# A recommendation tower on one core: a third table split into halves, the first dense part and one batch of transposes moved, the gather indices loaded on another queue

## The chip, the cores and the metric

One core of one Trainium2 chip runs the kernel. The metric is the device time of one execution in microseconds (us).

## The reference

512 samples each take one row of 128 floats from each of 26 tables, and have one dense vector of 128 features. The 27 vectors of a sample are multiplied with each other pairwise (351 dots), and dense vector and dots go through three layers.

```python
e = jnp.stack([tbl_0[ids[:, 0]], ..., tbl_25[ids[:, 25]]], axis=1)
ss = jnp.einsum('bfd,bgd->bfg', e, e); sd = jnp.einsum('bfd,bd->bf', e, dense)
z = concatenate([dense, sd, ss[:, iu, ju]], axis=1)           # iu, ju: pairs above the diagonal
h = concatenate([z, dense], axis=1)                            # 607 columns
h = maximum(h @ W_top1 + b_top1, 0)                            # 512
h = maximum(h @ W_top2 + b_top2, 0)                            # 256
y = h @ W_top3                                                 # 1
```

## The kernel before

The kernel holds the looked-up vectors transposed, as embT: 128 dimensions on the partitions, then sample, then slot (27 slots, padded to 32).

Twelve of the tables (1000 or 1250 rows) are looked up by a product with a one-hot matrix. Each of them is loaded whole over SP's DMA queue (load_table), ACT rounds it to fp32r (the high part, split_high, L324), DVE takes the remainder (the low part, split_low, L386) and compares the indices with each of 8 (once 10) chunk numbers (onehot, L378), and TensorE adds up 16 (once 20) products of a chunk's high and low part with the one-hot columns (L472). Buffers for table, high, low, onehot and the PSUM result exist three times (STAGES). ACT then copies the result into its slot of embT (L335). The step of a table is called T0 to T11; the semaphore table_selected counts finished products, table_placed the copies into embT.

The other 14 tables are gathered by GpSimd with an indirect DMA each, for each of 4 tiles of 128 samples: 56 gathers, numbered k = 14 t + n, into rows (two buffers, for even and odd tiles). k up to 42 are also paced by table_selected, and gathers named in HELD_BY_DOTS wait until the dots of an earlier tile are done. What is gathered is transposed by TensorE four tables at a time (the batches B t.b, L507; the last batch of a tile has two tables), and ACT or DVE copies a batch from PSUM into embT (L308, L371).

Then, for each tile t: TensorE makes the dots (D t, L527, 128 products); ACT and DVE copy them from PSUM into pairs, 22 copies each, in two parts of 11 (C t.0 and C t.1, L308 and L371); the first layer is the dense part (P t, 8 products, L543) and the pairs part (L t.0, L t.1, L552, 32 products); ACT applies the relu (R t, L349); the second layer (M t, L569), its relu (H t, on ACT and DVE), the third (Y t, L576) and the copy of the result (V t) follow. D t waits for all copies of C t-1, since the dots of all tiles share four PSUM banks, and for the batches of its tile in embT.

Every engine walks the same written list (STEPS) and does its part of each step, in order; between engines there are semaphores alone. A table with an entry in `late` is split: its first 256 samples are selected in step T t.0 ahead of D0, the other 256 in steps T t.1 to T t.4 (L485, 16 products) behind D0, into a PSUM region of their own, and ACT copies that half into embT in step A t (L338). Before, this holds for the last two tables (10 and 11). Table 10's late half goes to last_layers, table 11's to half of hidden[1].

Before the tables, TensorE runs some warming products, and spread_ids copies the indices of a table to all partitions with a product (L445).

Of the kernel before, what the change touches and what calls it, by code (L numbers as in the profile page):

```python
# [31 lines left out]
N_ONEHOT = len(ONEHOT_TABLES)  # L32
# [17 lines left out]
def dlrm_tower(nc, gather_ids, onehot_ids, spread, tables, dense_t, w_pairs, w_dense, small, w2, identity,  # L50
# [9 lines left out]
    GATHERS_AHEAD, GATHERS_PER_TABLE = 4, 3  # L60

    LATER_GATHERS = GATHERS_AHEAD + GATHERS_PER_TABLE * (N_ONEHOT + 1)
    HELD_BY_DOTS = {39: 1, 46: 2, 51: 3}
    WARMING = 29
    WARMING_BETWEEN = 6
    CHUNKS1 = HIDDEN1 // 128
# [3 lines left out]
    with ctx:  # L70
        def sb(name, shape, dt=F32):
            return ctx.enter_context(nc.sbuf_tensor(name, shape, dt))

        def pb(name, shape):
            return ctx.enter_context(nc.psum_tensor(name, shape, F32))

        def sem(name):
            return ctx.enter_context(nc.semaphore(name))

        gather_idx = sb("gather_idx", [128, TILES, N_GATHERED], I32)  # L80
# [26 lines left out]
        hidden = [pb(f"hidden{i}", [128, CHUNKS1, TILE]) for i in range(2)]  # L107
        last_layers = pb("last_layers", [128, 512])
        HALF_BATCH = BATCH // 2
# [2 lines left out]
        relative = banks[2:4]  # L112
        selected = [banks[0], banks[1], hidden[0].rearrange("p a b -> p (a b)")]

        late = {N_ONEHOT - 2: last_layers[:, 0:HALF_BATCH],
                N_ONEHOT - 1: hidden[1][:, 0:2, :].rearrange("p a b -> p (a b)")}

# [5 lines left out]
        gather_ids_loaded = sem("gather_ids_loaded")  # L124
# [19 lines left out]
        table_placed = sem("table_placed")  # L144
# [30 lines left out]
        def lows_to(i, chunk):  # L175

            return 2 * i + 1 + chunk // half(i)

        def loads_of(i):
# [3 lines left out]
        NAMES = {"T": "table", "D": "dots", "C": "copies", "B": "batch", "P": "dense", "L": "layer1", "R": "relu1",  # L183
                 "M": "layer2", "H": "relu2", "Y": "layer3", "V": "result", "A": "late half"}
        STEPS = [(NAMES[w[0]], *map(int, w[1:].split("."))) for w in """
            T0 T1 B0.0 T2 B0.1 T3 T4 B0.2 T5 B0.3 T6 B1.0 T7 B1.1 T8 B1.2 T9 B1.3 T10.0 T11.0 B2.0
            D0 C0.0 T10.1 T10.2 T10.3 T10.4 A10 T11.1 T11.2 T11.3 T11.4 C0.1 P0 B2.1 B2.2 A11
            D1 C1.0 B2.3 L0.0 L0.1 R0 C1.1 P1 B3.0 M0 H0
            D2 Y0 C2.0 V0 B3.1 L1.0 L1.1 R1 C2.1 P2 B3.2 M1 H1 B3.3
            D3 Y1 C3.0 V1 L2.0 L2.1 R2 C3.1 P3 M2 H2  # L190
            L3.0 Y2 V2 L3.1 R3 M3 H3 Y3 V3""".split()]
# [12 lines left out]
        def batch_placer(n):  # L204
            return PLACERS[n]
# [10 lines left out]
        @block.sync  # L216
        def _(sp):
            def load_rows(i, first, last, done):
                rows_of_part = tables[ONEHOT_TABLES[i]][:, :].rearrange("(p c) d -> p c d", c=CHUNKS[i])
                for a, b in ROW_PIECES:  # L220
                    sp.dma_start(table[i % TABLE_BUFFERS][a:b, first:last, :], rows_of_part[a:b, first:last, :]
                                 ).then_inc(done, 16)

            def load_table(i):
                if i >= TABLE_BUFFERS:
                    sp.wait_ge(low_ready, lows_to(i - TABLE_BUFFERS, CHUNKS[i - TABLE_BUFFERS] - 1))
                load_rows(i, 0, CHUNKS[i], table_loaded[i % TABLE_BUFFERS])

            def load_weights(n):
                dst, src = MLP_LOADS[n]  # L230
                sp.dma_start(dst, src).then_inc(mlp_loaded, 16)

            sp.dma_start(spread_f[0:ID_ROWS, :], spread).then_inc(spread_loaded, 16)
            for n, (first, last) in enumerate(parts(0)):
                load_rows(0, first, last, first_loaded[n])
            load_table(1)
            load_table(2)
            sp.dma_start(ident[:, :], identity).then_inc(ident_loaded, 16)
            load_table(3)
            load_table(4)  # L240
            sp.dma_start(denseT[:, :], dense_t).then_inc(dense_loaded, 16)
            load_table(5)
            for i in range(6, N_ONEHOT):
                load_table(i)
                if i - 6 < len(MLP_LOADS):
                    load_weights(i - 6)
            sp.wait_ge(y_ready, TILES)
            sp.dma_start(out, y).then_inc(stored, 16)
            sp.wait_ge(stored, 16)

        @block.gpsimd
        def _(pool):
# [4 lines left out]
            for t in range(TILES):  # L257
                for n in range(N_GATHERED):
# [3 lines left out]
                    if GATHERS_AHEAD + GATHERS_PER_TABLE <= k < LATER_GATHERS:  # L262
                        pool.wait_ge(table_selected, (k - GATHERS_AHEAD) // GATHERS_PER_TABLE)
                    if k in HELD_BY_DOTS:
                        pool.wait_ge(dots_done, HELD_BY_DOTS[k])
                    if t >= 2 and n % BATCH_T == 0:
# [38 lines left out]
        @block.scalar  # L305
        def _(act):
            def copy(dst, src):
                return nc.scalar.copy(dst, src)  # L308

            def relate_ids(i):  # L310
                act.wait_ge(ids_spread, i + 1)
                if i >= ID_BUFFERS:
                    act.wait_ge(onehot_ready, onehots_to(i - ID_BUFFERS, CHUNKS[i - ID_BUFFERS] - 1))
                nc.scalar.copy(ids_h[:, i % ID_BUFFERS, :], relative[i % 2][0:ROW_PARTS, :]).then_inc(ids_relative, 1)  # L314

            def split_high(i):
                for n, (first, last) in enumerate(parts(i)):
                    if i == 0:
                        act.wait_ge(first_loaded[n], 16 * len(ROW_PIECES))
                    else:  # L320
                        act.wait_ge(table_loaded[i % TABLE_BUFFERS], 16 * len(ROW_PIECES) * loads_of(i))
                    if i >= STAGES:
                        act.wait_ge(table_selected, i - STAGES + 1)
                    nc.scalar.copy(high[i % STAGES][:, first:last, :], table[i % TABLE_BUFFERS][:, first:last, :]  # L324
                                   ).then_inc(high_ready, 1)

            def step(kind, t, i=0):
                if kind == "table" and i == 0:
                    if t + IDS_AHEAD < N_ONEHOT:
                        relate_ids(t + IDS_AHEAD)  # L330
                    if t + STAGES < N_ONEHOT:
                        split_high(t + STAGES)
                    act.wait_ge(table_selected, t + 1)
                    samples = slice(0, HALF_BATCH if t in late else BATCH)
                    nc.scalar.copy(embT[:, samples, t], selected[t % STAGES][:, samples]).then_inc(table_placed, 1)  # L335
                elif kind == "late half":
                    act.wait_ge(table_selected, t + 1 + len(late))
                    nc.scalar.copy(embT[:, HALF_BATCH:BATCH, t], late[t]).then_inc(table_placed, 1)  # L338
                elif kind == "batch" and batch_placer(batch_no(t, i)) == 0:
                    place_batch(act, copy, 0, t, i)  # L340
                elif kind == "copies":
                    copy_dots(act, copy, 0, t, i)
                elif kind == "relu1":
                    for n in range(2):

                        act.wait_ge(layer1_done, 2 * (t + 1) if t < TILES - 1 else 2 * t + 1 + n)
                        blocks = slice(CHUNKS1 // 2 * n, CHUNKS1 // 2 * (n + 1))
                        bank = turned if t == TILES - 1 and n == 1 else hidden[t % 2]
                        nc.scalar.activation(h1[:, t % 2, blocks, :], bank[:, blocks, :], ACT.Relu  # L349
                                             ).then_inc(h1_ready, 1)  # L350
                elif kind == "relu2":
                    act.wait_ge(layer2_done, CHUNKS2 * t + 1)
                    nc.scalar.activation(h2[:, t % 2, 0, :], last_layers[:, 0:TILE], ACT.Relu,
                                         bias=b2s[:, 0:1]).then_inc(h2_ready[0], 1)

            act.dma_start(ids_i[:, :], onehot_ids).then_inc(onehot_ids_loaded, 16)
            act.dma_start(gather_idx[:, :, :], gather_ids).then_inc(gather_ids_loaded, 16)
            act.wait_ge(zeros_ready, 1)
            nc.scalar.activation(warmed[:, :], zeros[:, :], ACT.Identity)
            act.wait_ge(onehot_ids_loaded, 16)  # L360
            nc.scalar.copy(ids_f[0:ID_ROWS, :], ids_i[:, :]).then_inc(ids_converted, 1)
            for i in range(IDS_AHEAD):
                relate_ids(i)
                split_high(i)
            for s in STEPS:
                step(*s)
# [66 lines left out]
        def _(pe):  # L433
# [19 lines left out]
            def step(kind, t, i=0):  # L453
# [37 lines left out]
                elif kind == "batch":  # L491
# [10 lines left out]
                        placer = batch_placer(previous)  # L502
                        pe.wait_ge(batch_placed[placer], placed_by(placer, previous + 1))
                    if bank == "L" and n > BEFORE_LATE:
                        pe.wait_ge(table_placed, N_ONEHOT + 1)
                    for m in range(BATCH_SIZE[i]):
                        last = nc.tensor.transpose(transposes_of(n)[:, m, :], rows[:, t % 2, BATCH_T * i + m, :],  # L507
                                                   ident[:, :])
# [21 lines left out]
                    last.then_inc(dots_done, 1)  # L530
                elif kind == "dense":
                    if t == 0:
                        pe.wait_ge(mlp_loaded, MLP_LOADED)
                        pe.wait_ge(weights_added, 1)
                    if t == 1:
# [117 lines left out]
```

## Time and profile before

| | us |
|---|---|
| median of 3 runs | 115.47 |
| the three runs | 115.47, 131.96, 114.88 |
| the profiled execution, its time | 115.17 |
| its span, first to last instruction | 113.4 |
| TensorE busy | 104.1 (92%) |
| VectorE (DVE) busy | 84.6 (75%) |
| ScalarE (ACT) busy | 67.6 (60%) |
| GpSimd (POOL) busy | 61.2 (54%) |

The span is 1.8 us shorter than the time of the same execution, which also holds what lies before the first and behind the last instruction. A busy TensorE isn't TensorE at its peak. Its granted clock was 1.000 over the span. All instants below are microseconds from the start of the span.

### The profile page before, as it was taken

The page shows a single profiled execution, that of the slowest core. Times are in us where ns is not written, and L with a number is a line of the kernel's source. Part 1 is how long each engine was busy: PE and PEld are TensorE (multiplying, and loading weights), DVE is VectorE, ACT ScalarE, POOL GpSimd, SP SyncE. Part 2 cuts the span into 40 slices and gives each one's busy share as a digit, 9 for nine tenths or more (in the row PEclk, how much of TensorE's full clock was granted, in tenths as well). Part 3 has the DMA queues.
Part 4 walks back from the last instruction along what each step waited for, and adds up shares of the span by engine and source line. Part 5 has one row for each costly group of instructions (what it writes and reads, how often), then busy time and mean ns, then how long its engine had stood idle before and what let it go on. Part 6 is the DMA issues. An engine that isn't in the chain of part 4 may idle for free.

```text
span 113.4 us, 2832 instructions
## 1 busy us (share of the span) xinstructions
PE 104.1 (92%) x1095; PEld 92.4 (81%) x1095; DVE 84.6 (75%) x230; ACT 67.6 (60%) x153; POOL 61.2 (54%) x62
## 2 busy tenths in 40 slices
PE   6999997399999999999999969997999969997993
PEld 6787885388888888889899959997989949896890
DVE  4699999999999999999914891699259840885002
ACT  4657349878595685949534992669053960848120
POOL 7577777788777777687762775573047400000000
DMA  3996999664999999931110112111002100000000
GB/s 85 264 260 123 255 222 267 139 209 129 304 253 302 227 304 263 210 81 46 46 55 23 46 49 67 33 51 46 6 0 67 49 6 6 0 0 0 0 6 1
DMA packets 5057, 12.75 MB, mean 112 GB/s; under 512 B 1690, under 2 KB 1818, under 8 KB 5044
## 3 DMA queue, kind: packets, MB, share of 16 engines
q1 hardware_dynamic: 3060, 8.80, 29.8%
q0 software_dynamic: 1792, 3.67, 13.0%
q8 instruction: 9, 0.15, 0.6%
q10 hardware_dynamic: 192, 0.09, 0.4%
q14 instruction: 4, 0.03, 0.1%
HBM read 12.56 MB, written 0.00 MB: 111 GB/s over the span
## 4 chain that ended last, share of the span: by engine, by line
PE 62%; DMA 9%; ACT 9%; POOL 7%; DVE 7%; issue 4%; ACTq 0%
PE dots L472 19%; PE dots L527 14%; PE hidden L552 11%; PE hidden L472 8%; ACT pairs L308 7%; DMA rows<-tbl,gather_idx 7%; POOL rows L268 7%; DVE pairs L371 5%; DMA gather_idx<-gather_ids 3%; PE turned L507 2%; PE turned L552 2%; PE last_layers L576 2%; ACT h L349 2%; PE last_layers L507 1%; PE dots L445 1%
## 5 line engine op out<-in xcount | busy, mean ns | idle before, releaser
L268 POOL DMA_INDIRECT rows<-tbl,gather_idx x56 | 58.3, 1040 | 27.6 <-issue 14.0
L378 DVE TENSOR_SCALAR onehot<-ids_h 125x512 fp32r<-125x512 f16 x98 | 36.5, 430 | 1.1 <-ACT ids_h L314 1.1
L371 DVE COPY pairs<-dots 27x128 f32<-27x128 f32 (+8 forms) x88 | 23.8, 270 | 16.7 <-PE dots L527 14.1
L308 ACT COPY pairs<-dots 27x128 f32<-27x128 f32 (+8 forms) x88 | 20.9, 237 | 15.9 <-PE dots L527 13.9
L472 PE MATMUL dots<-onehot,high 125*128 125x512 f32 (+1 forms) x66 | 24.8, 396 | 0.0
L472 PE MATMUL dots<-onehot,low 125*128 125x512 f32 (+1 forms) x66 | 23.6, 378 | 0.0
L324 ACT CAST high<-table 125x1024 fp32r<-125x1024 f32 (+2 forms) x13 | 13.1, 1004 | 14.2 <-DMA table<-tbl 12.4
L527 PE MATMUL dots<-embT 128*64 128x54 f32 x512 | 15.8, 223 | 2.7 <-DVE pairs L371 1.0
L527 PEld LDWEIGHTS dots<-embT 128*64 128x64 f32 x512 | 15.4, 138 | 3.5 <-issue 2.5
L386 DVE TENSOR_TENSOR low<-table,high 125x512 fp32r<-125x512 f32 (+1 forms) x24 | 16.6, 690 | 0.0
L472 PEld LDWEIGHTS dots<-onehot,low 125*128 125x128 f32 x66 | 12.4, 189 | 2.3
L472 PEld LDWEIGHTS dots<-onehot,high 125*128 125x128 f32 x66 | 12.4, 189 | 2.2
L552 PE MATMUL hidden<-pairs,wp 128*128 128x128 f32 x112 | 13.4, 277 | 0.8 <-ACT pairs L308 0.8
L552 PEld LDWEIGHTS hidden<-pairs,wp 128*128 128x128 f32 x112 | 12.8, 192 | 1.3 <-ACT pairs L308 1.3
L472 PE MATMUL hidden<-onehot,high 125*128 125x512 f32 (+1 forms) x32 | 11.9, 382 | 0.0
L472 PE MATMUL hidden<-onehot,low 125*128 125x512 f32 (+1 forms) x32 | 11.3, 363 | 0.0
L335 ACT COPY embT<-dots 128x512 f32<-128x512 f32 (+1 forms) x8 | 8.5, 1066 | 0.0
L314 ACT CAST ids_h<-dots 125x512 f16<-125x512 f32 x12 | 7.5, 623 | 0.8 <-PE dots L445 0.8
L308 ACT COPY embT<-turned 128x512 f32<-128x512 f32 x7 | 7.9, 1128 | 0.0
L472 PEld LDWEIGHTS hidden<-onehot,low 125*128 125x128 f32 x32 | 6.1, 189 | 0.9
L472 PEld LDWEIGHTS hidden<-onehot,high 125*128 125x128 f32 x32 | 6.1, 189 | 0.8
L451 PE MATMUL last_layers<-zeros 128*128 128x128 f16 x47 | 5.4, 300 | 1.0 <-DVE zeros L421 1.0
(55 smaller groups left out, 104.6 us busy)
## 6 DMA issues: line engine op xcount, KB each, us to landing
table<-tbl SPq DMA_DIRECT2D x10, 448.0 KB
wp<-w_pairs SPq DMA_DIRECT2D x2, 512.0 KB, 7.5
rows<-tbl,gather_idx POOLq DMA_INDIRECT x56, 4.1
table<-tbl SPq DMA_DIRECT2D x1, 560.0 KB
table<-tbl SPq DMA_DIRECT2D x10, 52.0 KB
wd<-w_dense SPq DMA_DIRECT2D x1, 512.0 KB, 6.1
w2s<-w SPq DMA_DIRECT2D x1, 512.0 KB, 6.3
table<-tbl SPq DMA_DIRECT2D x2, 224.0 KB
```

The costliest lines, as they stand in the source:

```text
L268: pool.indirect_dma_start(out=rows[:, t % 2, n, :], out_offset=None, in_=tables[GATHERED_TABLES[n]][:, :], in_offset=bass.IndirectOffsetOn ...
L308: return nc.scalar.copy(dst, src)
L314: nc.scalar.copy(ids_h[:, i % ID_BUFFERS, :], relative[i % 2][0:ROW_PARTS, :]).then_inc(ids_relative, 1)
L324: nc.scalar.copy(high[i % STAGES][:, first:last, :], table[i % TABLE_BUFFERS][:, first:last, :]).then_inc(high_ready, 1)
L335: nc.scalar.copy(embT[:, samples, t], selected[t % STAGES][:, samples]).then_inc(table_placed, 1)
L371: return nc.vector.tensor_copy(dst, src)
L378: nc.vector.tensor_scalar(onehot[i % STAGES][:, c, :], ids_h[:, i % ID_BUFFERS, :], float(c), None, ALU.is_equal).then_inc(onehot_ready, 1)
L386: nc.vector.tensor_tensor(low[i % STAGES][:, first:last, :], table[i % TABLE_BUFFERS][:, first:last, :], high[i % STAGES][:, first:last, : ...
L451: nc.tensor.matmul(last_layers[:, 0:128], zeros[:, :], zeros[:, :], start=True, stop=True)
L472: last = nc.tensor.matmul(selected[t % STAGES][:, samples], part[t % STAGES][:, c, :], onehot[t % STAGES][:, c, samples], start=(part is h ...
L527: last = nc.tensor.matmul(dots[64 * h:64 * (h + 1), g, 0:2 * SLOTS], embT[:, s:s + 2, :].rearrange("p u s -> p (u s)"), embT[:, s:s + 2, 0 ...
L552: last = nc.tensor.matmul(hidden_block(t, m), wp[:, c, cols(m)], pairs[:, t % 2, c, :], start=False, stop=(c == PAIR_CHUNKS - 1), skip_gro ...
```

## The change

- Table 9 becomes a third split table. Step T9.0 selects its first 256 samples ahead of D0; T9.1 to T9.4 (16 products) and the copy A9 stand behind D0, ahead of those of tables 10 and 11. The late half uses half of the PSUM bank hidden[0].
- The first dense part P0 writes into hidden[0] too, so it waits for table_placed 13 (A9) and moves from ahead of D1 to behind D1 and B2.3.
- The second batch B0.1 moves from behind T2 to behind T3, and B1.3 from behind T9 to behind T10.0.
- The gathers that are held: k = 36, 43 and 50 wait for the dots of tiles 0, 1 and 2, where it was k = 39, 46 and 51.
- The load of the gather indices moves from second on ACT's queue to first on SP's, ahead of spread_f and the tables.
- A wait of the batches that use last_layers counts table_placed one higher.

```diff
-    HELD_BY_DOTS = {39: 1, 46: 2, 51: 3}
+    HELD_BY_DOTS = {36: 1, 43: 2, 50: 3}
...
-        late = {N_ONEHOT - 2: last_layers[:, 0:HALF_BATCH],
+        late = {N_ONEHOT - 3: hidden[0][:, 0:2, :].rearrange("p a b -> p (a b)"),
+                N_ONEHOT - 2: last_layers[:, 0:HALF_BATCH],
                 N_ONEHOT - 1: hidden[1][:, 0:2, :].rearrange("p a b -> p (a b)")}
...
-            T0 T1 B0.0 T2 B0.1 T3 T4 B0.2 T5 B0.3 T6 B1.0 T7 B1.1 T8 B1.2 T9 B1.3 T10.0 T11.0 B2.0
-            D0 C0.0 T10.1 T10.2 T10.3 T10.4 A10 T11.1 T11.2 T11.3 T11.4 C0.1 P0 B2.1 B2.2 A11
-            D1 C1.0 B2.3 L0.0 L0.1 R0 C1.1 P1 B3.0 M0 H0
+            T0 T1 B0.0 T2 T3 B0.1 T4 B0.2 T5 B0.3 T6 B1.0 T7 B1.1 T8 B1.2 T9.0 T10.0 B1.3 T11.0 B2.0
+            D0 C0.0 T9.1 T9.2 T9.3 T9.4 A9 T10.1 T10.2 T10.3 T10.4 A10 T11.1 T11.2 T11.3 T11.4 C0.1 B2.1 B2.2 A11
+            D1 C1.0 B2.3 P0 L0.0 L0.1 R0 C1.1 P1 B3.0 M0 H0
             D2 Y0 C2.0 V0 B3.1 L1.0 L1.1 R1 C2.1 P2 B3.2 M1 H1 B3.3
...
+            sp.dma_start(gather_idx[:, :, :], gather_ids).then_inc(gather_ids_loaded, 16)
             sp.dma_start(spread_f[0:ID_ROWS, :], spread).then_inc(spread_loaded, 16)
...
             act.dma_start(ids_i[:, :], onehot_ids).then_inc(onehot_ids_loaded, 16)
-            act.dma_start(gather_idx[:, :, :], gather_ids).then_inc(gather_ids_loaded, 16)
...
                     if bank == "L" and n > BEFORE_LATE:
-                        pe.wait_ge(table_placed, N_ONEHOT + 1)
+                        pe.wait_ge(table_placed, N_ONEHOT + 2)
...
                 elif kind == "dense":
                     if t == 0:
+                        pe.wait_ge(table_placed, N_ONEHOT + 1)
                         pe.wait_ge(mlp_loaded, MLP_LOADED)
```

## Rows read from the trace of the kernel before

**Rows 1.** The chain that ended last, in time: start, us, what.

```profile
21.63 0.66 PE last_layers L507 x4
...
48.34 3.68 PE dots L472 x16
...
52.24 1.92 PE dots L472 x16
...
56.12 0.60 ACT embT L335
...
56.85 3.96 PE dots L527 x128
```

**Rows 2.** Busy time by stretch: each engine's us (instructions), clock, DMA share, GB/s.

```profile
core 0: us, PE busy (x) PEld busy (x) DVE busy (x) ACT busy (x) POOL busy (x), PEclk, DMA share, GB/s
15.00:25.00 10.00, 7.57 (x38) 6.09 (x36) 10.00 (x26) 7.78 (x9) 7.87 (x8) 1.00 0.87 219
...
35.00:45.00 10.00, 10.00 (x50) 8.34 (x49) 10.00 (x26) 6.61 (x9) 7.33 (x7) 1.00 1.04 275
```

**Rows 3.** Timeline of DVE, table stage: start, us, what [idle before].

```profile
5.55 1.43 DVE L378 TENSOR_SCALAR onehot<-ids_h 125x512 fp32r<-125x512 f16 x4 [1.06 <-ACT ids_h L314]
...
54.19 1.14 DVE L378 TENSOR_SCALAR onehot<-ids_h 125x512 fp32r<-125x512 f16 x3
```

**Rows 4.** Timeline of PE, the last chunk of T11.0.

```profile
55.68 0.28 PE L472 MATMUL hidden<-onehot,high 125*128 125x256 f32 x1
```

**Rows 5.** Timeline of DVE, ACT and PE between D0 and D1.

```profile
60.83 6.59 DVE L371 COPY pairs<-dots 27x128 f32<-27x128 f32 x22 [3.83 <-PE dots L527]
...
63.81 0.64 ACT L338 COPY embT<-last_layers 128x256 f32<-128x256 f32 x1
64.48 2.75 ACT L308 COPY pairs<-dots 23x32 f32<-23x32 f32 x11
...
64.65 1.06 PE L543 MATMUL hidden<-denseT,wd 128*128 128x128 f32 x8
...
67.57 3.97 PE L527 MATMUL dots<-embT 128*64 128x54 f32 x128 [0.99 <-DVE pairs L371]
```

**Rows 6.** The chain in time, D1 to D2.

```profile
71.91 3.59 PE hidden L552 x32
75.52 0.66 ACT h L349 x2
...
79.20 3.94 PE dots L527 x128
```

**Rows 7.** Timeline of POOL: gathers k = 39, 40, 51 and 55.

```profile
61.56 0.94 POOL L268 DMA_INDIRECT rows<-tbl,gather_idx  x1 [2.32 <-PE dots L527]
62.81 0.94 POOL L268 DMA_INDIRECT rows<-tbl,gather_idx  x1 [0.30 <-issue]
...
83.42 0.94 POOL L268 DMA_INDIRECT rows<-tbl,gather_idx  x1 [5.66 <-PE dots L527]
...
88.41 0.94 POOL L268 DMA_INDIRECT rows<-tbl,gather_idx  x1 [0.30 <-issue]
```

**Rows 8.** The gathers' line, 83 to 90: from issue to landing.

```profile
DMA to landing us min/median/max: 2.5/2.5/2.6
```

**Rows 9.** Timeline of PE and DVE, D2 to D3.

```profile
88.59 0.66 PE L507 MATMUL turned<-ident,rows 128*128 128x128 f32 x4
...
91.40 0.41 PE L507 MATMUL dots<-ident,rows 128*128 128x128 f32 x2 [0.37 <-ACT pairs L308]
...
91.84 0.62 DVE L371 COPY embT<-dots 128x256 f32<-128x256 f32 x1 [0.41 <-PE dots L507]
...
92.56 3.95 PE L527 MATMUL dots<-embT 128*64 128x54 f32 x128 [0.76 <-DVE embT L371]
```

**Rows 10.** Timeline of ACT, POOL and DVE, the start.

```profile
3.48 0.62 ACT L361 CAST ids_f<-ids_i 32x512 f16<-32x512 int32 x1 [0.21 <-DMA ids_i<-onehot_ids]
4.64 1.09 POOL L268 DMA_INDIRECT rows<-tbl,gather_idx  x1 [1.16 <-DMA gather_idx<-gather_ids]
...
8.62 1.06 ACT L324 CAST high<-table 125x1024 fp32r<-125x1024 f32 x1 [0.76 <-DMA table<-tbl]
...
10.30 0.68 DVE L386 TENSOR_TENSOR low<-table,high 125x512 fp32r<-125x512 f32 x1
```

## The prediction

> **What bounds the kernel now.** I read the chain of waits first. Up to D0 it is a row of TensorE products with one hole, 2.4 us ahead of 21.63, where batch B0.1 waits for its gathers [rows 1]. The chain thus offers two gains: fill the hole, and take products out from ahead of D0. But a chain follows one path and doesn't show how near the next one is, so I read the busy time by stretch. In the table stage TensorE has a hole between 15 and 25, yet DVE was busy 10.00 of 10.00 us there, and again 10.00 of 10.00 between 35 and 45 [rows 2]. DVE's timeline says the same without a break: it waits once, for its first instruction at 5.55, and from there to the last one-hot compare of table 11, 54.19 to 55.33, no idle time stands before any of its groups [rows 3]. So two engines finish the tables almost together. TensorE's last chunk of T11.0 starts at 55.68 [rows 4], 0.35 us after DVE has made that chunk's one-hot. TensorE had fallen behind in the hole and made up for it later, with the halved tables. The reader is to see that each of the two engines would end the stage near 56, whatever happens to the other.
>
> Behind D0 I read, between each pair of dots, which wait ends last. D1 waits for DVE's 22 copies (60.83 to 67.42), with TensorE idle for 0.99 us; ACT's own copies end at 67.23, since A10 (0.64) lies between its two parts [rows 5]. D2 follows the chain L0, relu, ACT's second 11 copies [rows 6]. D3 waits for the last batch B3.3 to be transposed and copied [rows 9]. Between D3 and the end nothing of the change is found.
>
> **The change part by part.** All terms are against the profiled execution (115.17 us, span 113.4); the median of the runs shown is 0.3 us more.
>
> *Table 9 halved, B0.1 later (ahead of D0).* TensorE loses 16 products of 512 columns and gets 16 of 256: 3.68 - 1.92 = 1.76 us [rows 1]. B0.1 behind T3 finds its gathers landed, so up to 2.4 us of the hole are filled as well. On TensorE alone that is 4.2 us. DVE, however, loses no instruction: it makes all one-hots and low parts of table 9 in full, as before. Its work from 5.55 on is a fixed row of instructions, and the last one-hot stays at 55.33. TensorE walks T3 to T11 closer behind DVE; T11.0's last chunk can start at 55.33 plus a semaphore's passage. I take 0.05 to 0.1 for that, and so 0.3 us of gain, with 0 and 0.35 as ends; more is had only if DVE itself runs faster. B1.3 (two transposes) falls into slack. D0 starts 0.3 us earlier.
>
> *Late halves, A9, held gathers (D0 to D1).* Counted from the end of D0, 60.83. TensorE now has 48 late products (3 x 1.92), B2.1 and B2.2 (0.44 each): 6.7 us, less than what follows. ACT: the first 11 copies end at +2.96, A9 at +3.6; A10 must wait for the second table's late products, 2 x 1.92 plus some tenth, +4.0, and ends at +4.65; its other 11 copies take 2.75 [rows 5] and end at +7.4, against +6.4 before. D1 then starts at about +7.55, where it was +6.74. A second path ends at the same place. B2.2 takes gathers k = 36 to 39. Three of them were issued ahead of D0 and are now held until D0 is done. k = 39 was issued 0.73 us after D0 at the first place in line; now k = 36 has that place, and k = 39 comes 3 x 1.25 later [rows 7], at +4.5. It lands 2.5 us after its issue [rows 8], +7.0, and the four transposes (0.44) end at +7.45. B2.2 stands ahead of D1 in TensorE's order, so D1 can't pass it. Either path gives +0.8 us. If k = 36 starts 0.28 after the dots, as k = 51 did (83.14 to 83.42), the gathers end earlier and ACT alone decides, with nearly the same result; ends 0.4 and 1.1.
>
> *P0 moved (D1 to D2).* Ahead of D1 its removal brings nothing, as TensorE wasn't last there (0.99 us idle). Behind D1 it stands ahead of L0, whose end releases relu and ACT's second copies, and these release D2. Its 8 products take 0.89 from start to start of the next group (64.65 to 65.54) [rows 5]. D1's end to L0's end grows from 3.96 to 4.85, while ACT had been waiting there already; the chain behind (0.66 relu, 11 copies, 0.25) [rows 6] is unchanged. M0 ends at about +8.0 and D2 starts at +8.55, so M0 stays hidden. +0.9 us, ends 0.6 and 1.0. The added wait for table_placed 13 costs nothing: A9 is over 8 us old by then.
>
> *k = 50 held in place of 51 (D2 to D3).* Behind D2 six gathers follow in place of five. k = 50 takes the start 0.28 us behind D2, k = 55 starts 5 x 1.25 later, +6.5, lands at +9.0. Before, B3.3 was transposed at 91.40, +8.26, limited by ACT's copies with the gathers just behind (k = 55 at 88.41, landed 90.9) [rows 7, 9]. It now starts at +9.05, +0.8 us, and its copy and D3 follow at the same distance [rows 9]. B3.2 (k = 50 to 53) also moves, from +5.45 to about +6.55, and M1 with it to +8.8, still ahead of B3.3. Ends 0.4 and 1.1. Between D1 and D2 the holding costs nothing: k = 45 lands at about +5.3 and B3.0 comes to it at +5.8.
>
> *Indices first on SP's queue.* The first gather waits 1.16 us for them [rows 10]; it will start some 0.5 us earlier. That gain lies in gathers only, and B0.1 no longer waits for any. Against it, spread_f and every piece of tables 0 to 2 is issued some 0.4 us later. The one-hot indices (ids_f at 3.48) still set DVE's start. The high part of table 1 waits for its load until 8.62 and ends at 9.68; its low part is made at 10.30, so 0.6 us of slack take up 0.4 [rows 10]. Zero, ends -0.2 and +0.5: a late table here would move the whole row of DVE.
>
 By it the D2 to D3 term would be 0.45 in place of 0.8 and the D0 to D1 term would stay with ACT, 0.4 us less in all. The measured 2.5 is used.
>
> **Sum.** -0.3 + 0.8 + 0.9 + 0.8 + 0 = +2.2 us: 115.17 + 2.2 = 117.4 us, 1.9% over the profiled execution and 1.7% over the median.
>
> **Rivals.** (a) TensorE, not DVE, sets the table stage; then D0 comes up to 4.2 us earlier, and the three terms behind it (2.5) remain: 115.17 - 4.2 + 2.5 = 113.5 us. For it speaks that the chain names TensorE all through; against it, that DVE shows no idle time in 49 us [rows 2, 3]. If only table 9's saving comes through, 1.76, the time is 115.9. 10% for both. (b) The stage works as I say, but the held gathers are less late, or the copies shift so that less is lost (terms at their lower ends, 0.4, 0.6 and 0.4, with -0.35): 116.2 us; 20%. Speaking for it: two of three terms rest on instants within 0.3 us of another path. (c) On the slower side: the first tables land late. If table 1's load moves by more than its 0.6 us of slack, because the index transfer and the earlier gathers also take bandwidth (the DMA share is 0.87 to 1.04 in the table stage [rows 2]), DVE stalls and nothing makes up for it; 1 us of it gives 118.4 us; 15%. It decides from 0.2 us beyond my 0.4 on. (d) My sum, 55%.
>
> **How the numbers follow.** The likeliest is 117.4, within 116.9 and 117.9. Two of ten are left out at the far ends of (a) and (c), so the range is 115.9 to 118.4. About 2% (2.3 us) is what a measurement of this kernel can tell from no change, so the line lies near 117.6. (d) lies around it with somewhat more than half below, (b) and the 115.9 case lie within, (c) beyond: faster 0.10, same 0.52, slower 0.38.
>
> **What would show it.** DVE's last one-hot compare still ends near 55.3, and TensorE shows short idle times in T9.0 to T11.0 with the hole at 19.2 gone: if DVE ends later, (c); if D0 starts below 56, (a). From D0's end to D1's start 7.5 in place of 6.74, with B2.2 waiting for its gathers or D1 for ACT's copies. From D1's end to D2's start 8.5 in place of 7.66. From D2's end to D3's start 10.2 in place of 9.42, with B3.3 waiting for the DMA. The prediction is wrong if DVE's row gets shorter by more than a few tenths, which I have no row for, or if the gathers behind the dots go out faster than every 1.25 us.

## The result and the profile after

The changed kernel takes 117.41 us (median of 5 executions), the kernel before 115.09 (5 executions). The ratio of the executions below 120 us is 1.018, with a 95% interval of 1.013 to 1.023. So it is slower, by about 2 us; whether the loss is above or below 2% isn't settled. The forecast was 117.4.

Two of the five executions of the changed kernel took 133.0 and 132.9 us, and in three of the four comparisons below all executions of the kernel before took 131 to 156 us; the traces of such executions show engines that stopped for some microseconds, or a gather that took 6 to 23 us to issue, so I read from them distances inside stretches without such a stop, and no time.

The profile of this section is from the changed kernel run once more (after_again2): time 116.78, span 115.0, 1.6 us more than the 113.4 of before.

Divided at the starts of the dots, the two traces compare so:

| | before | changed | difference | forecast |
|---|---|---|---|---|
| start of D0 | 56.85 | 55.83 | -1.0 | -0.3 |
| D0's end (ACT's copies start) to D1's start | 60.83 to 67.57, 6.74 | 59.81 to 67.51, 7.70 | +1.0 | +0.8 |
| D1's end to D2's start | 71.54 to 79.20, 7.66 | 71.45 to 80.01, 8.56 | +0.9 | +0.9 |
| D2's end to D3's start | 83.14 to 92.56, 9.42 | 83.95 to 94.17, 10.22 | +0.8 | +0.8 |
| D3's start to the end | 20.84 | 20.83 | 0 | 0 |

With two decimals the differences sum to 1.63 us; D1 itself took 0.03 less, and the spans differ by 1.6. The trace of one of the 133 us executions, clean behind D0, has the same three distances: 7.67, 8.57 and 10.20.

The end of the table stage, first DVE's timeline (start, us, what, idle before), for [rows 3]:

```profile
4.92 1.49 DVE L379 TENSOR_SCALAR onehot<-ids_h 125x512 fp32r<-125x512 f16 x4 [0.42 <-ACT ids_h L316]
...
10.12 0.69 DVE L387 TENSOR_TENSOR low<-table,high 125x512 fp32r<-125x512 f32 x1 [0.33 <-ACT high L326]
...
53.41 1.08 DVE L379 TENSOR_SCALAR onehot<-ids_h 125x512 fp32r<-125x512 f16 x3
```

and TensorE's, for [rows 4] and the last row of [rows 1]:

```profile
46.28 0.66 PE L508 MATMUL turned<-ident,rows 128*128 128x128 f32 x4 [1.20 <-DMA rows<-tbl,gather_idx]
...
51.94 0.39 PE L473 MATMUL hidden<-onehot,low 125*128 125x256 f32 x1 [0.42 <-DVE low L387]
...
53.54 0.38 PE L473 MATMUL hidden<-onehot,low 125*128 125x256 f32 x1 [0.15 <-DVE low L387]
...
54.55 0.38 PE L473 MATMUL hidden<-onehot,high 125*128 125x256 f32 x1
...
55.83 3.94 PE L528 MATMUL dots<-embT 128*64 128x54 f32 x128 [0.33 <-ACT embT L337]
```

The hole of 2.4 us ahead of B0.1 is gone. A smaller one has come, 1.20 us at 46.28, where B1.2 waits for its gathers (the last, k = 25, was issued at 38.85 and landed 7.4 us later); TensorE makes up for it in the halved tables that follow. It now waits in T11.0 for DVE's low parts, by name. In T11.0 the last chunk starts 0.06 us after the compare that feeds it has ended (53.41 + 1.08 = 54.49); before it was 0.35. DVE's row starts 0.63 earlier and ends 0.84 earlier. It has one wait more, 0.33 at 10.12. So of the 1.13 that the last chunk starts earlier (55.68 to 54.55), 0.84 is DVE's row and 0.29 is TensorE following closer.

Behind D0, ACT, TensorE and POOL, for [rows 5] and the first two of [rows 7]:

```profile
62.80 0.64 ACT L340 COPY embT<-hidden 128x256 f32<-128x256 f32 x1
63.84 0.64 ACT L340 COPY embT<-last_layers 128x256 f32<-128x256 f32 x1 [0.40 <-PE last_layers L486]
64.50 2.75 ACT L310 COPY pairs<-dots 23x32 f32<-23x32 f32 x11
```

```profile
66.77 0.66 PE L508 MATMUL last_layers<-ident,rows 128*128 128x128 f32 x4 [0.60 <-DMA rows<-tbl,gather_idx]
67.51 3.94 PE L528 MATMUL dots<-embT 128*64 128x54 f32 x128
```

```profile
60.53 0.94 POOL L270 DMA_INDIRECT rows<-tbl,gather_idx  x1 [7.50 <-issue]
...
64.28 0.94 POOL L270 DMA_INDIRECT rows<-tbl,gather_idx  x1 [0.30 <-issue]
```

Both paths of the prediction are there. A9 (62.80) and A10 (63.84, waiting 0.40 for its products) push ACT's second copies to 67.25. k = 36 starts at 60.53 and k = 39 at 64.28; 2.49 later B2.2 starts, after 0.60 of waiting for it. D1 starts when both ACT's copies (67.25) and B2.2 (67.43) have ended.

D1 to D2, ACT and TensorE, for [rows 6]:

```profile
76.33 0.66 ACT L351 ACTIVATE h<-hidden 128x256 f32<-128x256 f32 x2 [1.87 <-PE hidden L554]
77.01 2.75 ACT L310 COPY pairs<-dots 23x32 f32<-23x32 f32 x11
```

```profile
71.66 1.06 PE L545 MATMUL hidden<-denseT,wd 128*128 128x128 f32 x8
72.55 3.74 PE L554 MATMUL hidden<-pairs,wp 128*128 128x128 f32 x32
```

P0 stands from 71.66 to 72.55 ahead of L0, 0.89, and ACT waits 1.87 for L0's end where it waited 0.97.

D2 to D3, TensorE and POOL, for [rows 9] and the end of [rows 7]:

```profile
90.46 0.66 PE L508 MATMUL turned<-ident,rows 128*128 128x128 f32 x4 [0.92 <-DMA rows<-tbl,gather_idx]
...
93.01 0.44 PE L508 MATMUL dots<-ident,rows 128*128 128x128 f32 x2
94.17 1.03 PE L528 MATMUL dots<-embT 128*64 128x54 f32 x28 [0.72 <-issue]
```

```profile
84.23 0.94 POOL L270 DMA_INDIRECT rows<-tbl,gather_idx  x1 [4.07 <-PE dots L528]
...
90.48 0.94 POOL L270 DMA_INDIRECT rows<-tbl,gather_idx  x1 [0.30 <-issue]
```

B3.2 waits 0.92 for k = 53. k = 55 is issued at 90.48; 93.01 is 2.53 later, the landing time of [rows 8]. M1's products end at about 92.75, so the gather is last by 0.25.

### The profile page after: what moved, and what is told of

Its sections match the earlier page's. It is cut to its first block and busy times, and to the rows that moved or that the text cites. A ratio compares the mean times of both kernels' runs of the same rounds, so it can differ in the third digit from the quotient of the medians.

```text
span 131.2 us, 2864 instructions
## 1 busy us (share of the span) xinstructions
PE 107.1 (82%) x1111; PEld 94.4 (72%) x1111; DVE 84.1 (64%) x230; ACT 68.2 (52%) x154; POOL 82.4 (63%) x62
## 5 line engine op out<-in xcount | busy, mean ns | idle before, releaser
L270 POOL DMA_INDIRECT rows<-tbl,gather_idx x56 | 79.5, 1420 | 24.7 <-issue 16.3
L379 DVE TENSOR_SCALAR onehot<-ids_h 125x512 fp32r<-125x512 f16 x98 | 36.2, 438 | 14.0 <-PE dots L473 13.6
L473 PE MATMUL dots<-onehot,high 125*128 125x512 f32 (+1 forms) x66 | 25.3, 407 | 0.0
L508 PE MATMUL turned<-ident,rows 128*128 128x128 f32 x38 | 6.5, 296 | 18.1 <-DMA rows<-tbl,gather_idx 18.1
L508 PEld LDWEIGHTS turned<-ident,rows 128*128 128x128 f32 x38 | 4.6, 149 | 19.6 <-DMA rows<-tbl,gather_idx 19.0
L473 PEld LDWEIGHTS dots<-onehot,low 125*128 125x128 f32 x66 | 13.2, 202 | 2.9 <-DVE low L387 0.7
L473 PEld LDWEIGHTS dots<-onehot,high 125*128 125x128 f32 x66 | 13.3, 202 | 2.4 <-DVE onehot L379 0.2
```

The costliest lines, as they stand in the source:

```text
L270: pool.indirect_dma_start(out=rows[:, t % 2, n, :], out_offset=None, in_=tables[GATHERED_TABLES[n]][:, :], in_offset=bass.IndirectOffsetOn ...
L379: nc.vector.tensor_scalar(onehot[i % STAGES][:, c, :], ids_h[:, i % ID_BUFFERS, :], float(c), None, ALU.is_equal).then_inc(onehot_ready, 1)
L473: last = nc.tensor.matmul(selected[t % STAGES][:, samples], part[t % STAGES][:, c, :], onehot[t % STAGES][:, c, samples], start=(part is h ...
```

## The experiments

**The changed kernel again**, no edit. The first time (after_again):

> The changed kernel itself, once more, for an undisturbed trace. My theory (the row of DVE instructions sets the table stage, and three waits behind D0 grow): D0 starts near 56.5 where it was 56.85, from D0's end to D1's start 7.5 us (was 6.74), from D1's end to D2's start 8.5 (was 7.66), from D2's end to D3's start 10.2 (was 9.42), the last one-hot compare still ends near 55.3; 117.4 us, ratio 1.018. The rival (DVE is delayed at the start by the loads issued later): the first part would show DVE idle before a low part, and its last one-hot compare later than 55.6, with less than 2 us behind D0.

145.41 us against 151.56 for the kernel before. Up to D0 its trace can be read: DVE's last compare ends at 54.51, ACT's copy of table 11's first half starts at 55.11 (56.12 before). The second time (after_again2):

> The changed kernel again, since the run of the same kernel before this one fell on a chip where the kernel before took 135 us and more. As there: D0 starts near 56.5, from D0's end to D1's start 7.5 us, D1's end to D2's start 8.5, D2's end to D3's start 10.2, ratio to the kernel before 1.018. The rival (DVE delayed at the start) would show DVE's last one-hot compare later than 55.6.

This is the trace above. Its four executions took 116.78, 118.68, 133.13 and 135.06 us, nine of the kernel before 114.70 to 134.29; the lowest differ by 2.1 us. The three distances came as expected; D0 came 0.7 us earlier than expected, and a part of the rival is there (DVE idle ahead of a low part, 0.33), but more than paid for.

**P0 put back ahead of D1**, twice.

```
-  ... T11.4 C0.1 B2.1 B2.2 A11 D1 C1.0 B2.3 P0 L0.0
+  ... T11.4 C0.1 P0 B2.1 B2.2 A11 D1 C1.0 B2.3 L0.0
```

> The changed kernel with the first dense part P0 put back ahead of B2.1 and D1. If P0 lies on the chain behind D1, D1's end to D2's start goes back from 8.5 to 7.66, 0.9 us. Ahead of D1 TensorE then has 3 x 1.92 + 0.89 + 0.88 = 7.5 us, as long as the other two paths: D1 stays or moves 0.1 us later. 116.6 us. The rival, that TensorE ahead of D1 is what the change relieved, gives 117.4 again: what is won behind D1 is lost ahead of it.

136.26 us against 151.56, not readable behind D0. The second:

> The changed kernel with the first dense part P0 put back ahead of B2.1 and D1. If P0 lies on the chain behind D1, D1's end to D2's start goes back from 8.5 to 7.66; ahead of D1 the three paths (ACT's copies with A9 and A10, the held gathers, TensorE's products) end together and D1 moves by 0.1 us at most: 0.8 us less than the changed kernel, ratio 1.011. The rival, that TensorE ahead of D1 is what the change relieved, gives the changed kernel's time again.

All four of its executions took 131.5 us and more; in the profiled one a gather took 23 us to issue (last section). Behind D0 its trace is clean. Its TensorE:

```profile
83.37 3.94 PE L528 MATMUL dots<-embT 128*64 128x54 f32 x128
87.25 0.44 PE L508 MATMUL turned<-ident,rows 128*128 128x128 f32 x2
87.53 3.74 PE L554 MATMUL hidden<-pairs,wp 128*128 128x128 f32 x32
...
94.99 3.94 PE L528 MATMUL dots<-embT 128*64 128x54 f32 x128
98.86 0.60 PE L578 MATMUL last_layers<-h,smalls 128*1 128x128 f32 x4
...
105.53 0.66 PE L508 MATMUL turned<-ident,rows 128*128 128x128 f32 x4 [1.02 <-DMA rows<-tbl,gather_idx]
```

D1 ends at 87.31 and D2 starts at 94.99: 7.68, where the changed kernel has 8.56 and the kernel before 7.66. The 0.9 us is P0's place, and nothing else. From D0's end (ACT's copies at 75.69) to D1 it is 7.68, as in the changed kernel (7.70), although P0 stands there again: TensorE ahead of D1 wasn't what the change relieved. From D2's end (98.93) to D3 (109.17) it is 10.24, still with a wait for the DMA ahead of B3.2.

**The gathers held as before**, twice, in the changed kernel.

```diff
-    HELD_BY_DOTS = {36: 1, 43: 2, 50: 3}
+    HELD_BY_DOTS = {39: 1, 46: 2, 51: 3}
```

> The changed kernel with the gathers held as before (39, 46, 51 in place of 36, 43, 50). If the held gathers cost what I said, D2's end to D3's start goes back to 9.4 (0.8 us less), and D0's end to D1's start stays near 7.5, since ACT's copies with A9 end there too: 116.6 us, 0.8 less than the changed kernel. If the gathers alone had set D1 as well, both come back: 115.8. If neither, no change.

> The changed kernel with the gathers held as before (39, 46, 51). D2's end to D3's start goes back from 10.2 to 9.4. From D0's end to D1's start it stays near 7.6: B2.2's wait for its gathers goes, but ACT's copies with A9 and A10 end only 0.1 us earlier. 0.9 us less than the changed kernel, ratio 1.008 to 1.010. If the gathers alone set both, 1.8 us less.

141.81 us and 143.51, with the kernel before at 151.56 and 151.22: no verdict by time. In the first trace TensorE's transposes of B3.2 follow the dense part without a wait:

```profile
102.46 1.06 PE L545 MATMUL hidden<-denseT,wd 128*128 128x128 f32 x8
103.35 0.65 PE L508 MATMUL turned<-ident,rows 128*128 128x128 f32 x4
```

They start 5.41 us behind D2's end (97.94), and in the second trace 5.41 behind it too (114.07 to 119.48), again without a wait; before it was 5.45. Held at 50, this batch waited 0.92 and 1.02 for the DMA and started 6.5 and 6.6 behind D2's end. So the wait ahead of B3.2 comes from the hold. That D3 would come back by 0.8 wasn't measured: in this trace ACT stopped for 4.5 us between D2 and D3.

**Both put back**, P0 and the hold.

> The changed kernel with P0 put back ahead of D1 and the gathers held as before (39, 46, 51), so that table 9's late half, the early index load and the later B0.1 remain. The late half then costs one term only: from D0's end to D1's start 7.6 us (ACT's copies with A9 and A10 end at 7.45, TensorE's products with P0 at 7.5), against 6.74 before. D1's end to D2's start is 7.65 and D2's end to D3's start 9.4, as before. With D0 at 55.85: 115.17 - 1.0 + 0.9 = 115.0 us, ratio 0.999. If the held gathers had cost nothing, D2 to D3 stays at 10.2 and the time is 115.8.

136.06 us against 139.96 (ACT stopped for 3.7 to 4.5 us in three places). Neither the total nor the distances behind D0 can be told.

**Parts of the change alone, on the kernel before.** First the index load:

```diff
+            sp.dma_start(gather_idx[:, :, :], gather_ids).then_inc(gather_ids_loaded, 16)
             sp.dma_start(spread_f[0:ID_ROWS, :], spread).then_inc(spread_loaded, 16)
...
-            act.dma_start(gather_idx[:, :, :], gather_ids).then_inc(gather_ids_loaded, 16)
```

> The kernel before with one part of the change: the gather indices loaded first on SP's queue. In the changed kernel's trace DVE's row starts at 4.92 in place of 5.55 and ends at 54.49 in place of 55.33. If the index load's place does that, DVE starts near 4.9 here too, the first gather starts near 3.65, TensorE's hole ahead of B0.1 shrinks by up to 1 us, and D0 starts 0.5 to 1.0 us earlier than 56.85, with nothing lost behind it: 114.2 to 114.7 us, ratio 0.992 to 0.996. The rival (what I had forecast): it moves gathers only, ratio 1.000.

142.2 us against 151.22; the ratio, 1.006 with 0.993 to 1.020, leaves it open. The first gather starts at 3.65 (4.64 before) and DVE's row at 5.12 (5.55 before); the row ends at 54.98 (55.33 before). TensorE's hole ahead of B0.1 is still there (2.60, to 21.61). I had expected the earlier gathers to shrink it, and they didn't: the last one that B0.1 takes, k = 7, was issued at 13.60 (14.17 before), but B0.1 started 8.0 us later in place of 7.5.

Then the index load and B0.1 behind T3 (T2 T3 B0.1 T4), twice, table 9 whole:

> The kernel before with the two parts of the change that lie at its start: the indices first on SP's queue, and B0.1 behind T3. Table 9 stays whole, P0 and the held gathers stay as before. If DVE's row sets the end of the table stage, halving table 9 adds nothing to these two: D0 starts near 55.85, as in the changed kernel, and the three distances behind it are those of before, 6.74, 7.66 and 9.42: 114.2 us, ratio 0.991, 3 us under the changed kernel. The rival (TensorE's saved 1.76 us made the gain): D0 stays at 56.3 or later.

> The kernel before with the indices first on SP's queue and B0.1 behind T3 alone; table 9 stays whole. As before: if DVE's row sets the end of the table stage, halving table 9 adds nothing to these two, and D0 starts near 55.9 with the three distances of before behind it (6.74, 7.66, 9.42): 114.2 us, ratio 0.991. The rival (TensorE's saved 1.76 us made the gain): D0 stays at 56.3 or later, ratio 0.996 or more.

137.99 and 136.24 us against 151.22 and 139.96, no verdict by time. In the second trace DVE's row has no wait in it, and TensorE follows it closely to the end of the tables; DVE, TensorE and ACT:

```profile
53.23 1.08 DVE L378 TENSOR_SCALAR onehot<-ids_h 125x512 fp32r<-125x512 f16 x3
```

```profile
53.36 0.38 PE L472 MATMUL hidden<-onehot,low 125*128 125x256 f32 x1 [0.15 <-DVE low L386]
```

```profile
54.91 0.59 ACT L336 COPY embT<-hidden 128x256 f32<-128x256 f32 x1 [1.62 <-PE hidden L472]
```

The copy of table 11's first half, the last thing before D0, starts at 54.91: 1.2 us earlier than before and 0.2 earlier than in the changed kernel (55.10), with table 9 not halved. With its 1.76 us of products still there TensorE waits for DVE's low part in T11.0, so the rival, that TensorE's saved 1.76 us made the gain, falls for this trace. (D0 itself is late there, since a gather was.) Two things limit it. A gather was stuck from 45.14 to 55.73, and beside a stuck gather no compare is lengthened (see the next experiment), so part of the 1.2 may be owed to that. And in the first trace, of the same kernel, DVE's row ends at 55.35, as before (with 0.33 us of waiting and five of the longest compares in it, against none and one in the second), and TensorE, which had waited 2.83 us ahead of B1.2 (to 48.32), was later still. The first trace shows the stretch behind D0 undisturbed up to D1, DVE and TensorE:

```profile
68.29 6.59 DVE L371 COPY pairs<-dots 27x128 f32<-27x128 f32 x22 [11.26 <-PE dots L527]
```

```profile
75.03 0.71 PE L527 MATMUL dots<-embT 128*64 128x54 f32 x13 [0.97 <-DVE pairs L371]
```

6.74 us from 68.29 to 75.03, with DVE's copies last as before; 6.74 in the second trace and 6.80 with the index load alone. Without table 9's late half and the earlier holds the 1.0 us of this stretch isn't there; the two weren't parted, and in the changed kernel's trace they end within 0.2 us of each other.

**DVE's row shortened.** The copy of the dense vectors (0.54 us) goes behind table 11's one-hots:

```diff
-                    if t == 2:
+                    if t + 1 == N_ONEHOT:
                         dve.wait_ge(dense_loaded, 16)
```

> The changed kernel with DVE's copy of the dense vectors into embT (0.54 us from start to start of the next) moved from behind the one-hots of table 3 to behind those of table 11, where DVE waits. No work is left out. If DVE's row sets the end of the table stage in the changed kernel, the last one-hot ends 0.54 earlier and D0 starts 0.5 earlier: 116.9 us. If TensorE sets it (the rival), D0 stays: 117.4.

> As the kernel with the two early parts, and DVE's copy of the dense vectors (0.54 us) moved behind the one-hots of table 11, where DVE waits. DVE's row then ends 0.5 earlier, near 54.0. With table 9 whole, TensorE's own products end near 54.7, so D0 comes only 0.2 us earlier than with the two parts alone: 114.0 us, ratio 0.989. If TensorE has more slack than that, 113.7.

136.28 against 151.56 and 138.7 against 151.22. The second has a gather stalled inside the table stage and tells nothing. In the first, DVE's row has no wait in it, and the trace contradicts me. Its DVE:

```profile
53.42 1.09 DVE L379 TENSOR_SCALAR onehot<-ids_h 125x512 fp32r<-125x512 f16 x3
54.43 0.70 DVE L401 COPY embT<-denseT 128x512 f32<-128x512 f32 x1
```

The last compare ends at 54.51, exactly where after_again, the changed kernel in the same comparison, has it, with the same start (5.36). The work taken out was given back: DVE's groups by line, from 5.36 to 54.4, busy us and mean ns, first the changed kernel

```profile
L379 DVE TENSOR_SCALAR onehot<-ids_h 125x512 fp32r<-125x512 f16 x98 | 35.6, 422 | 0.9 <-issue 0.9
```

and then with the copy moved:

```profile
L379 DVE TENSOR_SCALAR onehot<-ids_h 125x512 fp32r<-125x512 f16 x98 | 36.2, 429 | 0.9 <-issue 0.9
```

The same 98 compares took 0.6 us more. It sits in single compares. From the start of one to the start of what follows it, a compare takes 0.33 to 0.34 us as a rule, but some take 0.06 more and some 0.13 more, and so a group of three takes 1.08, 1.14 or 1.21. What goes with it stands on GpSimd's timeline. One such group of the kernel before, and the same one of the changed kernel (after_again2), each with the gather beside it:

```profile
36.37 1.21 DVE L378 TENSOR_SCALAR onehot<-ids_h 125x512 fp32r<-125x512 f16 x3
```

```profile
35.48 1.18 POOL L268 DMA_INDIRECT rows<-tbl,gather_idx  x1 [0.54 <-PE hidden L472]
```

```profile
36.05 1.08 DVE L379 TENSOR_SCALAR onehot<-ids_h 125x512 fp32r<-125x512 f16 x3
```

```profile
34.91 1.09 POOL L270 DMA_INDIRECT rows<-tbl,gather_idx  x1 [0.30 <-issue]
```

The gather's issue ends at 36.66 in the first, 0.29 us after the compare has started; in the second it ends at 36.00, just ahead of the compare. Compare by compare, the fourteen traces have 205 lengthened ones outside stuck gathers, and in 194 of them a gather's issue ends. In 162 it ends 0.22 to 0.24 us after the compare's start, and they take 0.38 to 0.40; in 32 it ends after 0.28 to 0.30, and they take 0.45 to 0.47. Of the other eleven, nine stand right behind the copy of the dense vectors. Where an issue ends earlier in a compare (18 of them) the compare isn't lengthened, and beside gathers that were stuck (last section) none of 208 is.

So the length of DVE's row goes with how many gathers end late in a compare. The kernel before has six of the long ones (0.13 more), the changed kernel (after_again2) one; with the copy moved there are five, against one in after_again, which besides had a gather stuck from 45.83 on. That accounts for the 0.6 us: the row didn't answer to the work taken out, it met the gathers otherwise. That DVE and GpSimd hold each other up there is read from the times alone; no run without gathers was made, and why an issue ends in one place or another wasn't found. TensorE's last chunk followed the last compare within 0.1 us here too.

## Why the prediction was right

**The table stage.** That the chain named TensorE while DVE set the stage nearly as late was right: TensorE waits for DVE's low parts in T11.0, with table 9 halved and, in one trace, with it whole. The size was off: 1.0 us in place of 0.3. Two terms failed. "The one-hot indices (ids_f at 3.48) still set DVE's start": with the indices off ACT's queue, where their issue took 0.45 us, ACT's first work starts at 1.19 in place of 1.67 and ids_f is converted at 2.84 (2.71 to 2.92 in all runs with that edit), and DVE's row starts at 4.92; the other runs with the edit start it between 4.94 and 5.47, before it was 5.55, so between 0.1 and 0.6 of it is to be had (those at 5.36 and 5.47 follow a stop of ACT). And "Its work from 5.55 on is a fixed row of instructions": it ran from 4.92 to 54.49, 49.57 with 0.33 of waiting, so 49.24 of work where it had been 49.78; ten groups of three compares alone took 10.1 us, from the start of each to the start of the next group, in place of 10.8. Five compares fewer that are 0.13 longer, as a gather's issue ends in them, cover that 0.5 (see the moved copy). I had written that the prediction would be wrong if the row got shorter by more than a few tenths, and it did, by 0.5. D0 at 55.83 also lies below the 56 that I had named as the sign of rival (a), TensorE setting the stage. The sign was badly chosen, as a DVE row that starts earlier and is shorter gives it too, and here TensorE waits for DVE by name. The mechanism of this term was thus incomplete. That the time still fell on the forecast is luck in part (see the sum).

**The rival of late first tables** was half there: table 1's high part ended at 10.09, 0.4 later, as worked out, but DVE came to it earlier, and the two together made the wait of 0.33.

**D0 to D1.** +1.0 in place of +0.8. Both paths ran as worked out, to within 0.1: k = 36 issued 0.72 after the dots, k = 39 at +4.47, ACT's copies ending at +7.44. Missed was the last step: D1 starts 0.26 after ACT's end (0.25 in two more traces), as D2 does before the change (78.95 to 79.20), not 0.15 as D1 does after DVE's (67.42 to 67.57).

**D1 to D2.** +0.9, shown by putting P0 back, in one trace.

**D2 to D3.** +0.8 as worked out, with k = 55's issue and landing on the spot. The wait ahead of B3.2 goes with the old hold; the whole distance is argued from the trace, not shown by removal. The measured landing of 2.5 us served; by the fit of the Trainium skill ("DMA: Bandwidth & Descriptors", Anatomy of one DMA — SWDGE (gpsimd) path), 2.15 us, k = 55 would have landed by 92.63; k = 53 would have landed 0.35 earlier too, and B3.2 and M1 with it, so that D3 would have come 0.35 earlier than it did, an estimate. The trace doesn't agree with that.

**The sum** was 117.4 and the median 117.41, but the profiled executions differ by 1.6, not 2.2: a gain three times the forecast stood against a slightly larger loss (2.7 in place of 2.5), and the medians of five lie 0.1 below and 0.6 above the profiled executions. The agreement of the totals is closer than that of the terms: the three terms behind D0 and the wait that sets each were forecast, the match to a tenth is luck.

The index load with B0.1 later, alone, is the part of the change that the traces speak for: in one of its two the table stage ends 1.2 us earlier, in the other DVE's row ends as before, and the one distance behind D0 that could be read, that to D1, doesn't grow. By those numbers it would take between 114.0 us (115.17 - 1.2) and 115.2, an estimate that no run without stops has confirmed.

## What to carry to other kernels

When a chain of waits names one engine through a stage, look whether another is busy without a break in the same stage. Work taken off the named engine then returns no more than what lies between the two (here 0.3 us; the rest of the 1.0 came from the other engine's own earlier start and shorter row), and where that work is put it can cost in full. In a written order, ask of each moved step what stands behind it on its own engine and which wait that step now precedes; P0, 0.9 us of products, was free in a stretch that waited for another engine and cost all of it ahead of the products that release the next one. A transfer held until an event lands a fixed sum later (here 0.3 to 0.7, plus 1.25 for each one ahead of it, plus 2.5 behind D0; in the table stage, from 30 to 50, the gathers took 2.8 to 7.6 us to land); count it against the first instruction that needs it.

## What the runs showed of the hardware that I had not expected

A gather's issue on GpSimd, 0.94 to 1.5 us as a rule, sometimes didn't end while DVE worked without a break. In the second run with P0 ahead, POOL and DVE:

```profile
24.77 23.05 POOL L270 DMA_INDIRECT rows<-tbl,gather_idx  x1 [0.30 <-issue]
```

```profile
59.25 0.76 DVE L379 TENSOR_SCALAR onehot<-ids_h 125x512 fp32r<-125x512 f16 x2 [12.26 <-PE dots L473]
```

The gather ended at 47.82. DVE had run out of work at 46.99 (59.25 - 12.26), as TensorE waited for the batch that takes that gather (k = 15) and the two behind it: 0.83 us earlier. A distance of 0.81 to 0.83 stands in six other traces too, at stalls of 6.2 to 23.0 us: DVE's first pause at 38.97 and the gather's end at 39.80, 46.11 and 46.92, 51.20 and 52.03, 54.92 and 55.73, 54.95 and 55.78, 55.11 and 55.94. The two profiled executions with a stall of 23 us took 131.8 and 133.0 us. The Trainium skill ("SBUF — State Buffer", Who interferes with whom) says that VectorE and GpSimd share a port pair as an exclusive lock, so that one is blocked wholly; that fits the end of each stall, but doesn't say by itself why the other gathers got through between the same DVE instructions. What makes one gather miss its turn is open.

A row of DVE instructions without any wait isn't of fixed length: the same 98 compares took 35.6 and 36.2 us in two kernels. A compare in which a gather's issue ends takes 0.06 us longer where that is 0.22 to 0.24 us after its start, and 0.13 longer where it is 0.28 to 0.30; beside stuck gathers none of 208 did.
